# A graph layer and an LSTM on one core: the products of the forget gates and the low parts of the recurrent weights formed by GpSimd instead of VectorE

## The reference

```python
combined = jnp.concatenate((x_t, h_prev), axis=1)
f_t = jax.nn.sigmoid(combined @ W_f + b_f)
i_t = jax.nn.sigmoid(combined @ W_i + b_i)
c_tilde = jnp.tanh(combined @ W_c + b_c)
c_t = f_t * c_prev + i_t * c_tilde
o_t = jax.nn.sigmoid(combined @ W_o + b_o)
h_t = o_t * jnp.tanh(c_t)
```

## Time and profile before

| | |
|---|---|
| median of 3 runs | 2661.74 us (2660.68 to 2664.11) |
| the profiled execution's own time | 2665.65 us |
| its span | 2664.1 us |
| rough round, first gate to last forget product | 1372.9 to 1579.1 us |
| kept round, first product to last forget product | 1584.6 to 2018.9 us |
| GpSimd busy in the span | 998.1 us, 37% |
| VectorE busy in the span | 2156.0 us, 81% |

### The profile page before, as it was taken

How to read it: one execution, slowest core, us unless ns; L and a number is a source line. 1 busy time by engine, 2 the same in 40 slices (tenths; PEclk the granted TensorE clock), 3 DMA queues, 4 the chain that set the end, 5 groups by cost and what they waited for, 6 DMA issues and landing times. The chain is left out here.

```text
span 2664.1 us, 47528 instructions
## 1 busy us (share of the span) xinstructions
PE 2514.0 (94%) x10745; PEld 1830.3 (69%) x10746; DVE 2156.0 (81%) x5780; ACT 1560.6 (59%) x3989; POOL 998.1 (37%) x1018
## 2 busy tenths in 40 slices
PE   7978999999999999999979999999998999989997
PEld 5865777777777777777756666666665556555554
DVE  7757888888888898888848877777777777778786
ACT  5655555555555555555536656666665777767775
POOL 1127777777777767777520000000000000023333
PEclk9997999999999999999989999999999999999998
DMA  9647998898988888888777747777777666499995
GB/s 236 189 134 230 296 277 253 263 278 257 276 267 267 264 246 279 274 257 264 232 208 199 195 121 237 244 237 237 236 243 209 167 168 169 137 235 251 252 250 144
DMA packets 194207, 611.15 MB, mean 229 GB/s; under 512 B 41822, under 2 KB 47966, under 8 KB 164394
## 3 DMA queue, kind: packets, MB, share of 16 engines
q1 hardware_dynamic: 120432, 370.08, 46.8%
q0 software_dynamic: 73712, 240.39, 31.7%
HBM read 468.71 MB, written 141.62 MB: 229 GB/s over the span
## 5 line engine op out<-in xcount | busy, mean ns | idle before, releaser
L834 POOL DMA_INDIRECT kept<-ln_table,kept x800 | 822.7, 1028 | 291.8 <-issue 208.4
L1548 PE MATMUL acc<-shared,state 128*125 128x512 f32 x2244 | 775.3, 416 | 63.5 <-DVE state L1867 48.8
L1548 PEld LDWEIGHTS acc<-shared,state 128*125 128x125 f32 x2244 | 401.6, 187 | 198.1 <-ACT acc L1477 67.6
L875 ACT ACTIVATE shared<-kept 128x512 fp32r<-128x512 f32 x800 | 441.3, 624 | 152.2 <-PE agg L928 109.4
L1387 POOL TENSOR_TENSOR out<-h,lx 125x512 f32<-125x512 f32 x50 | 64.5, 1290 | 1107.7 <-DVE h L1892 1107.7
L928 PE MATMUL agg<-shared,onehot 128*125 128x512 f32 x1200 | 377.4, 408 | 21.7 <-DVE shared L1045 18.6
L1548 PE MATMUL acc<-W_low,state 128*125 128x512 f32 x800 | 316.5, 396 | 0.0
L1548 PE MATMUL acc<-last_high,state 128*125 128x512 f32 x748 | 298.7, 399 | 0.0
L928 PEld LDWEIGHTS agg<-shared,onehot 128*125 128x125 f32 x1200 | 225.5, 189 | 98.5 <-DVE low_part L1045 16.8
L1045 DVE TENSOR_TENSOR low_part<-kept,shared 128x512 fp32r<-128x512 f32 x400 | 265.7, 693 | 10.8 <-ACT shared L875 4.3
L1045 DVE TENSOR_TENSOR shared<-kept,shared 128x512 fp32r<-128x512 f32 x400 | 259.3, 688 | 16.3 <-ACT shared L875 10.5
(11 more groups left out here) (237 smaller groups left out, 4379.4 us busy)
## 6 DMA issues: line engine op xcount, KB each, us to landing
xg<-total_rows SPq DMA_DIRECT2D x100, 896.0 KB
xg<-gate_rows SPq DMA_DIRECT2D x88, 896.0 KB
gate_rows<-gout SPq DMA_DIRECT2D x200, 224.0 KB
total_rows<-total SPq DMA_DIRECT2D x50, 896.0 KB
kept<-ln_table,kept POOLq DMA_INDIRECT x800, 4.5
lx<-x_rows POOLq DMA_DIRECT2D x50, 250.0 KB, 7.3
out_dram<-out POOLq DMA_DIRECT2D x50, 250.0 KB, 2.9
held<-in_x_dram SPq DMA_DIRECT2D x25, 448.0 KB
```

The lines of the kernel that those rows point to most:

```text
L834: e.indirect_dma_start(out=rows[j % RING][:, :], out_offset=None, in_=table[:, :], in_offset=bass.IndirectOffsetOnAxis(ap=ends[:, b, j, 0: ...
L875: e.activation(high[j % PARTS][:, :], rows[j % RING][:, :], ACT.Copy).then_inc(s_high, 1)
L1548: m = e.matmul(acc[n][0:L, :], stationary[:, k, :], weights[k][:, n * PAIR:(n + 1) * PAIR], start=begins, stop=(k == K - 1), skip_group_ch ...
```

## The change

GpSimd gets a `steps` for the rough and the kept round. Per step it waits for both halves of the forget gates (`s_fi`) and for its last product, multiplies the whole 125 x 512, and in the 36 inner steps of the rough round forms the 194 columns of `W_low` behind it. Its four pieces of the fourth chunk move from ahead of the rough round to behind that round's last step. VectorE loses `decayed` in the two rounds and `weights_low`. VectorE's wait at the end of the rough round is for the cleared tiles alone; TensorE's wait at the start of the kept round, for all pieces, is as before.

```diff
@@ gpsimd
             e.memset(decay[:, :, :], 1.0).then_inc(s_clear, 1)
-            e.wait_ge(s_init, 1)
-            for n in range(LAST_PIECES):
-                at, to = slice(n * PAIR, (n + 1) * PAIR), slice((K - 1) * G4 + n * PAIR, (K - 1) * G4 + (n + 1) * PAIR)
-                e.tensor_tensor(W_low[:, to], Wh_flat[:, to], last_high[:, at].bitcast(F32),
+            e.wait_ge(s_clear, CLEARED)
+
+            def weights_low(s):
+                e.wait_ge(s_clear, s - (SKIP + 1) + CLEARED)
+                at = bass.ds((s - (SKIP + 1)) * APART, PIECE)
+                e.tensor_tensor(W_low[:, at], Wh_flat[:, at], shared[:, at].bitcast(F32),
                                 ALU.subtract).then_inc(s_clear, 1)
 
+            def last_weights_low():
+                e.wait_ge(s_init, 1)
+                for n in range(LAST_PIECES):
+                    at, to = slice(n * PAIR, (n + 1) * PAIR), slice((K - 1) * G4 + n * PAIR, (K - 1) * G4 + (n + 1) * PAIR)
+                    e.tensor_tensor(W_low[:, to], Wh_flat[:, to], last_high[:, at].bitcast(F32),
+                                    ALU.subtract).then_inc(s_clear, 1)
+
             def steps(r, kind):
+                if kind in ("rough", "kept"):
+                    gates, faded = (r_gate, r_decay) if kind == "rough" else (gate, decay)
+
+                    def decayed(s, q, first, last):
+                        now = r * STEPS + s + (AHEAD + 1)
+                        for half in range(2):
+                            e.wait_ge(s_fi[half], now)
+                        e.wait_ge(s_decay, now - 1)
+                        e.tensor_tensor(faded[0:L], faded[0:L], gates[0:L, :, 0, 0], ALU.mult).then_inc(s_decay, 1)
+                        if kind == "rough" and not first and not last:
+                            weights_low(s)
+                    steps_of_round(e, kind, decayed)
+                    if kind == "rough":
+                        last_weights_low()
                 if kind not in ("final", "more"):
                     return
@@ vector
-                    def weights_low():
-                        at = bass.ds((s - (SKIP + 1)) * APART, PIECE)
-                        e.tensor_tensor(W_low[:, at], Wh_flat[:, at], shared[:, at].bitcast(F32),
-                                        ALU.subtract).then_inc(s_clear, 1)
-
@@ rough
                             to_state(SECOND)
-                        if kind == "rough":
-                            decayed()
                         if not last:
                             seed()
-                        if kind == "rough" and not first and not last:
-                            weights_low()
@@ measure
                 if kind == "rough":
-                    e.wait_ge(s_clear, CLEARED + PIECES + LAST_PIECES)
+                    e.wait_ge(s_clear, CLEARED)
```

## The result

The changed kernel takes 2749.66 us, median of 4 runs (2747.36 to 2754.66), against 2661.81 before: ratio 1.0331, 95% interval 1.0319 to 1.0343. It is slower by 88 us, where 100 were forecast, and inside the range. The profiled execution took 2747.36 us, span 2745.8.

A forecast was written before the change was run, and what follows sets the result against it. TensorE alone was taken to bound rough steps, a chain through TensorE, VectorE, sigmoid and cell the kept ones. 59.0 + 5.7 + 35.1 = 99.8 us on 2665.65 gives 2765.5, or 2761.5 on the median; range 2718 to 2800.

The forecast's parts named there:

- The mechanism: Both rounds: a VectorE instruction with two SBUF inputs waits out a GpSimd instruction that reads SBUF; 99.8 us in all.
- The 62.6 us taken from VectorE: Forget products and W_low pieces removed from VectorE in both rounds; predicted gain 0, except 0.4 us at the rough round's end.
- Rival B: Both rounds: GpSimd works beside VectorE with no contention that costs, 2661 us; chance 0.04.
- C: Rough steps: relieving VectorE's queue ahead of the cell product takes off up to 28 us, 2634; chance 0.03.
- D: TensorE's granted clock falls too with late h: half the rough steps 2830 us, all 2900; chance 0.06.
- A: Both rounds: hold partly hidden, rough delay 0.7 to 1.1 us a step, kept 0.4, about 2717 us; chance 0.11.
- Rough inner step: 36 inner rough steps: first h waits for GpSimd's product and piece, 1.64 us late each, 59.0 us.
- Kept step: Kept round: second-half cell product held by GpSimd's product, 0.77 us late, 0.70 after slack; 35.1 us with first and last.
- the 0.07 of slack: Kept steps: TensorE's time in hand before loading the last h, about 0.1 us, counted as 0.07 at its middle.
- The last kept step, counted with 0.77: Kept round's end: cell product 0.77 us late, with no slack at TensorE deducted.
- Last rough step: Rough round's end: product and four pieces hold VectorE 6.2 us ahead of last h and correction; net cost 5.7 us.
- its sum would differ by under 5 us: Claim for a lock letting VectorE in after each GpSimd instruction, instead of a hold over several: total changes under 5 us.

The follow-up runs named there:

- the late kernels: GpSimd's product started after the step's last h: in the changed kernel 2665.44 us; with only the kept product moved from the kernel before, ratio 0.9998.
- e7_added_fills: Kernel before, VectorE keeping its work, plus two GpSimd fills of unused tiles per rough and kept step: 2663.31 us, ratio 1.0002.
- e6_added_product: Kernel before, VectorE keeping its work, plus a GpSimd product of an unused tile per rough and kept step: 2720.84 us, ratio 1.0219.
- e8_kept_late: Kernel before with only the kept round's forget product on GpSimd, started after the step's last h: 2661.90 us, ratio 0.9998.
- e9_kinds_beside: Kernel with the late kept product, plus a second GpSimd product and small VectorE instructions of four kinds per kept step; only instruction lengths used, no kernel time given.
- e10_no_signal: Same small VectorE instructions beside three GpSimd products per kept step, the first raising no semaphore: 2687.02 us in one run against 2663.66.
- e3_pieces_only: Kernel before with only the W_low pieces of the 36 inner rough steps on GpSimd: 2673.19 us, ratio 1.0033.

## Why the prediction was right, and where its terms were off

The mechanism was right: it was named before the run, and the runs show it. The 62.6 us taken from VectorE gave nothing: the late kernels show it. The cost is VectorE's wait for GpSimd's reads, and it falls on the two instructions named, `h` in the rough round and the cell product in the kept one. The sizes were less good than the total looks. Rival B (no contention) and C (faster) fall with e7_added_fills, e6_added_product and e8_kept_late; D (the clock) falls too, since the granted clock stayed 1.00 with TensorE 84% busy. A (partly hidden) would have needed a kept delay of 0.4, and it is 0.87. In the rough round, though, the measured delay of 1.14 us a step stands next to A's upper end of 1.1 and far from the forecast's 1.64: not for A's reasons, since next to nothing of the hold falls into idle time; the hold itself was taken too long.

The sum came out 12 us high: 18.0 too much in the rough steps, 1.6 too much in the last of them, and 7.3 too little in the kept ones. That the errors partly cancel is luck.

*Rough inner step, 1.64 forecast, 1.14 measured (41.0 us for 59.0).* Two things were mis-sized. The hold: I had GpSimd wait for VectorE's cell product and begin 0.32 us after the sigmoid; it began 0.12 after it, beside that product, and the hold ended at 1477.21, 1.88 us after the sigmoid's end (1475.33), not 2.13. And the order: I had the first `h` wait for product and piece, but it got in between them, and only the second `h` waited for the piece. That one ended 1.96 after the sigmoid where it used to end 0.72 after it (1475.44 against 1474.72 in the earlier trace rows): 1.24 late, of which 0.1 is made up before the next product (L1571). Of the two lengths the float16 product was too high (1.27 for 1.21) and the piece too low (0.54 for 0.59).

*Kept step, 0.70 forecast, 0.87 measured (42.4 for 35.1).* GpSimd began 0.14 after the sigmoid, not 0.07, so the hold ended 0.07 later. And the 0.07 of slack that I granted TensorE is not there in most steps. The kept steps go in fours, three of 8.57 us and one of 8.66, and the earlier trace rows show the long one. In that one TensorE has 0.08 in hand; in the others its load of `h` (L1568) was waiting for `h` before the change already, in 37 waits over the 48 steps from 1600 to 2010 us:

```profile
PEld hturn L1568 <- DVE h L1892: 13.8, 37, 0.4
```

0.70 + 0.07 + 0.07 = 0.84, and that is what a step of 8.57 (now 9.41) or a long one (now 9.50) got later; in the changed kernel two of four are long, which gives the last 0.02. Why they are is not shown. The last kept step, counted with 0.77, comes 1.9 late at the next round, as said below the stage table.

*Last rough step, 5.7 forecast, 4.1 measured.* The first `h` did not wait for all five GpSimd instructions; VectorE did one instruction behind each. The correction's first subtraction came 4.8 us later (2.2 us after that `h` before, 7.0 after), and 0.7 came back behind it, in the first products of the kept round. In 15.5 us from the first of them on the granted clock was 0.82 before and 0.88 after, a mix of its two levels, 1.2 and 2.4 GHz, with more of the higher:

```profile
1584.50:1600.00 15.50, 15.25 (x55) 11.26 (x56) 6.86 (x21) 5.10 (x18) 0.00 (x0) 0.82 0.25 76
...
1624.60:1640.10 15.50, 14.32 (x54) 10.53 (x55) 6.97 (x20) 5.10 (x18) 1.29 (x1) 0.88 0.27 86
```

In choosing the hold for several GpSimd instructions I followed the 4.61 us of the earlier trace rows in the rough step too. The Trainium skill, SBUF — State Buffer, section "Who interferes with whom", has the lock held for one whole instruction, and that is what the changed kernel, e9_kinds_beside and e10_no_signal show. The forecast's sentence that its sum would differ by under 5 us was wrong for the inner step: the 0.2 us between first and second `h`, 36 times, is 7 us by itself.

What that section of the Trainium skill says of writes agrees too: a VectorE instruction with two SBUF inputs does not wait for a GpSimd instruction that only writes (e7_added_fills, no added us). The Trainium skill's words there on the order, that whichever is first keeps the other out, are not settled by these traces for the case of VectorE first. GpSimd's float16 product starts in the record beside a running cell product and is 0.06 us longer when the two overlap by 0.2 instead of 0.08 (1.208 for 1.144), and a piece beside a running `h` takes 0.64 for 0.59. That would fit a wait inside its length, but one shorter than the overlap.

## What to carry to other kernels

Before work goes from VectorE to GpSimd, look at what VectorE does in the microsecond in which GpSimd would run: if GpSimd reads SBUF, each of VectorE's instructions with two SBUF inputs was held to the end of the GpSimd instruction here, and so were small copies and additions within SBUF. GpSimd work belongs under VectorE's work on PSUM, or under its waits; one wait changed was worth 84 us here. And ask first whether the engine to be relieved is late for anything: 0.77 us a step that end when the next input arrives are worth nothing.

## What the runs showed of the hardware that was not expected

A GpSimd product with the same tile as both inputs, written to another tile, takes 1.04 us for 125x512 float32, where the one that multiplies a tile by another in place takes 1.29. In place, a float16 GpSimd product of that size takes 1.14 to 1.21 us, less than the float32 one of 1.29, though with one tile as both inputs float16 is no faster (1.08 against 1.04), and fills of the two types take the same. A `W_low` piece of 194 columns takes 0.59 on end with the product and 0.64 alone in e3_pieces_only, where it overlaps VectorE's `h`. And a copy of 125x2 elements with a single input is held by GpSimd just like a product of two tiles.
